# A decoder layer in one kernel: unread products and reordered loads ahead of the first tokens, five instead of four query projections ahead of the output projection

## The reference

```
x = x + attention(layernorm(x))           # 32 query heads, 8 key/value heads, rope, causal, out projection, biases
x = x + quantise(layernorm(x)) @ quantise(ctx[b])      # 0..255 levels, two scales and zero points
x = x + base(layernorm(x)) + lora          # x @ W_org.T + routed mixture: down (8x64), softmax weights, up
```

## Time and profile before

| | us |
|---|---|
| median of 3 runs (lowest, highest) | 791.65 (790.46, 792.01) |
| profiled execution | 793.04 |
| its span | 791.2 |

### The profile page before, as it was taken

One profiled execution on the slowest core, in us unless ns is written; L12 is line 12 of the kernel. 1 busy time (PEld: TensorE's weight loads), 2 busy tenths in 40 slices (PEclk: granted clock), 3 DMA queues, 4 the chain that ended last, 5 costly groups with the idle time before them and its releaser, 6 DMA issues.

```text
span 791.2 us, 12919 instructions
## 1 busy us (share of the span) xinstructions
PE 693.7 (88%) x4608; PEld 556.9 (70%) x4608; DVE 421.7 (53%) x1123; ACT 429.9 (54%) x1025; POOL 307.6 (39%) x384
## 2 busy tenths in 40 slices
PE   3999599999999899998768687799996787799998
PEld 3897477788777677875546475588875666588886
DVE  3366377776777536656648353433336569831212
ACT  3325378878787667797665653646314660512320
POOL 5337655543342534471304710505713011525510
PEclk9998899999999999999979698999999797699999
DMA  7504856563445606225350430403425342323102
GB/s 251 193 2 159 245 174 170 157 172 97 136 121 177 201 23 189 64 75 163 112 164 1 130 75 4 120 14 108 160 88 179 100 148 85 120 93 107 41 13 94
DMA packets 43823, 93.49 MB, mean 118 GB/s; under 512 B 5488, under 2 KB 5872, under 8 KB 42224
## 3 DMA queue, kind: packets, MB, share of 16 engines
q1 hardware_dynamic: 40176, 76.94, 30.2%
q0 software_dynamic: 3584, 15.73, 8.3%
HBM read 72.72 MB, written 19.92 MB: 117 GB/s over the span
## 4 chain that ended last, share of the span: by engine, by line
PE 58%; DVE 15%; POOL 9%; ACT 8%; issue 6%; DMA 2%; SPq 1%; DVEq 0%; ACTq 0%
PE dense L1023 37%; PE probt L917 7%; PE score L905 5%; PE pv L932 4%; POOL w_lo L1558 3%; PE score L1023 2%; DVE stats L1295 2%; DVE prob_all L1251 2%; ACT stage L1060 2%; ACT prob_all L1104 2%; POOL ln_s L828 2%; DVE act_t L1318 1%; POOL prob_all L1575 1%; POOL ln_s L830 1%; DVE prob_all L1344 1%
## 5 line engine op out<-in xcount | busy, mean ns | idle before, releaser
L1023 PE MATMUL dense<-w_hi,act_t 128*128 128x512 f32 (+1 forms) x684 | 233.4, 404 | 23.6 <-DVE act_t L1318 10.7
L1251 DVE CUSTOM_DVE_ANT_0 prob_all<-score,mask_sb 128x128 f32<-128x128 f32 (+3 forms) x256 | 123.7, 487 | 141.4 <-PE score L905 139.5
L1558 POOL TENSOR_TENSOR w_lo<-stage,w_hi 128x512 fp32r<-128x512 f32 x89 | 116.4, 1316 | 191.5 <-ACT w_hi L1064 191.2
L1104 ACT ACTIVATE prob_all<-prob_all,neg_max 128x128 f32<-128x128 f32 (+3 forms) x256 | 143.2, 559 | 72.4 <-DVE neg_max L1251 70.6
L1023 PEld LDWEIGHTS dense<-w_hi,act_t 128*128 128x128 f32 x684 | 133.3, 200 | 51.8 <-DVE act_t L1318 11.8
L1023 PE MATMUL dense<-w_lo,act_t 128*128 128x512 f32 (+1 forms) x372 | 138.5, 393 | 5.6 <-DVE xres L1389 3.1
L1023 PE MATMUL dense<-act_t,w_hi 128*128 128x512 f32 x408 | 139.6, 424 | 1.8 <-DVE xres L1367 1.8
L917 PE MATMUL probt<-ident_sb,prob_all 128*128 128x128 f32 x640 | 113.9, 277 | 1.4 <-ACT prob_all L1113 1.1
L905 PE MATMUL score<-k_stack,q_stack 96*128 96x128 f32 (+3 forms) x256 | 92.1, 364 | 13.9 <-DVE neg_max L1251 7.5
L1064 ACT ACTIVATE w_hi<-stage 128x512 fp32r<-128x512 f32 x117 | 71.9, 624 | 50.9 <-PE dense L1023 31.1
L1113 ACT ACTIVATE prob_all<-probt 128x128 f32<-128x128 f32 (+3 forms) x160 | 68.2, 426 | 47.0 <-PE probt L917 46.0
(11 more groups left out here) (156 smaller groups left out, 916.0 us busy)
## 6 DMA issues: line engine op xcount, KB each, us to landing
q_stack<-rope_dram POOLq DMA_DIRECT2D x16, 768.0 KB, 7.4
stage<-in_w_qk SPq DMA_DIRECT2D x40, 256.0 KB, 3.0
rope_dram<-act_t SPq DMA_DIRECT2D x40, 256.0 KB, 3.3
stage<-in_w_o SPq DMA_DIRECT2D x32, 256.0 KB, 3.0
stage<-in_ctx_kv SPq DMA_DIRECT2D x24, 256.0 KB, 3.1
stage<-in_w_org SPq DMA_DIRECT2D x24, 256.0 KB, 2.8
xres<-in_x SPq DMA_DIRECT2D x8, 512.0 KB, 6.6
prob_all<-in_x SPq DMA_DIRECT2D x8, 512.0 KB, 6.8
```

The costliest lines, as they stand in the source:

```text
L1023: last = engine.matmul(dst, lhs, rhs, start=(k == 0 and c == 0), stop=(k == g.kts - 1 and c == len(pairs) - 1))
L1104: engine.activation(prob[:, u % P_SLOTS, 0:length], prob[:, u % P_SLOTS, 0:length], ACT.Exp, bias=neg_max[:, m:m + 1], scale=-1.0, accum_o ...
L1251: engine.tensor_tensor_reduce(prob[:, u % P_SLOTS, 0:length], score_bank[u % 2][:, 0:length], mask_sb[:, S - length:S], -1.0, HIGHEST, ALU ...
L1558: engine.tensor_tensor(slot_lo(p, 0, NW), raw_of(p), slot_hi(p, 0, NW).bitcast(F32), ALU.subtract).then_inc(g_piece, 1)
```

## The change

- `keep_clock`: PE runs 16 matmuls of 512 columns on a zeroed tile (in q_stack) into dense bank 0 before the first turn. No one reads them.
- Norm (1,0) has its chains on DVE. SP issues the loads of token tiles 1, 2, 3 later, and the key weights earlier. ACT and DVE have tile 0's norm first, and the rest in a new order.
- In slots 0 to 2 the turn of the next token tile stands in the middle of the 24 steps, not behind them.
- The query projection 4 of half 1 stands ahead of `out` 0; before it stood between `out` 0 and `out` 1.
- `PV_LAG`: product with the values one slot later, and with it all that follows (sum's transposes, scaling, attention's parts).
- In units: cross pieces are rounded a slot after their scaling; DVE has the maximum and the probability copy ahead of the token copies. Four low pieces of `base` 0 of half 0 go from POOL to DVE.
- Outside units, a turn needs its source 5.0 us of the plan earlier (`LATE_TURN_US`), not 1.2, so it stands behind more steps; DVE has the second quantising step first in its slot.

```diff
+PV_LAG = 5
+BLANKS = 16
+LATE_TURN_US = 5.0
-CHAINS_ON_VECTOR = ((2, 1), (3, 1))
+CHAINS_ON_VECTOR = ((1, 0), (2, 1), (3, 1))
...
-        for g in range(NKV - LATE_ROPES):
+        for g in range(NKV - LATE_ROPES + 1):
             self.whole("q", 1, g, [0], KD, S, 4)
         self.whole("out", 0, 0, self.TILES, KD, NW, 1)
...
             if cross:
-                self.note("round", j, p)
+                self.note("round", j + 1 if unit else j, p)
...
-        return p < 8 and p % 2 == 1 or ... or piece["kind"] == "out" and p % 2 == 1
+        return p < 8 and p % 2 == 1 or ... or piece["kind"] == "base" and piece["b"] == 0 and piece["nb"] == 0 and p % 2 == 1
...
-                if not self.past(j, source, 3 if unit else 1, now, 1.2):
+                if not self.past(j, source, 3 if unit else 1, now, 1.2 if unit else LATE_TURN_US):
...
             fetch(1)
+            fetch(2)
             load_x(0, 1)
-            fetch(2)
             fetch(3)
-            load_x(0, 2)
             engine.dma_start(bias_v[:, :], b_v.to_broadcast([P, VW])).then_inc(d_bv, 16)
             fetch(4)
             fetch(5)
-            load_x(0, 3)
             fetch(6)
             fetch(7)
+            load_x(0, 2)
+            load_x(0, 3)
...
+            def keep_clock():
+                e.wait_ge(v_blank, 1)
+                for _ in range(BLANKS):
+                    engine.matmul(dense_bank[0][:, :], blank[:, 0:P], blank, start=True, stop=True)
...
-                if j < NT:
+                if j == 0:
+                    keep_clock()
                     for half in range(2):
-                        turn_tokens(1, 0, j, half)
+                        turn_tokens(1, 0, 0, half)
...
                 for s in range(first, end):
+                    if j < NT - 1 and s == first + plan.token_steps // 2:
+                        for half in range(2):
+                            turn_tokens(1, 0, j + 1, half)
...
-                if 0 <= u - 4 < UNITS and (u - 4) % GROUP == GROUP - 1:
-                    values((u - 4) // GROUP)
+                if 0 <= u - PV_LAG < UNITS and (u - PV_LAG) % GROUP == GROUP - 1:
+                    values((u - PV_LAG) // GROUP)
```

More of the change, by code:

```diff
@@ L391, in due_norms @@
                     self.note("turn", j, (which, b, t, half))
-                    self.note("tokens", j + 1 if unit else j, (which, b, t, half))
+                    self.note("tokens", j + TOKENS_LAG if unit else j, (which, b, t, half))
                     halves.append(j)
@@ L1458, in vector_program @@
                 u = j - first_unit
+                if j < NT - 1:
+                    for half in range(2):
+                        tokens_low(1, 0, j + 1, half)
                 if j < NT - 2:
@@ L1461, in vector_program @@
                         norm_stats(1, 0, j + 2, part)
-                if j < NT - 1:
-                    for half in range(2):
-                        tokens_low(1, 0, j + 1, half)
                 if j == NT + 2:
@@ L1468, in vector_program @@
                     constants()
+                if 0 <= u < UNITS:
+                    maximum(u)
+                if 0 <= u - 3 < UNITS and probt_on[u - 3] == "vector":
+                    take_out_turned(u - 3)
+                if not 0 <= u < UNITS:
+                    for b, t in at["second"].get(j, ()):
+                        quantise_second(b, t)
                 for which, b, t, half in at["tokens"].get(j, ()):
```

54 lines of the change are left out of this document (31 added, 23 removed).

## The result

| | before | after |
|---|---|---|
| median of the runs compared (lowest, highest) | 791.83 (790.46, 793.52) | 759.29 (757.09, 764.01) |
| profiled execution, span | 793.04, 791.2 | 760.35, 758.6 |

The ratio is 0.960 [0.954, 0.965], 32.5 us.

What follows compares the result with a forecast made beforehand. PE was taken as full in places, with order able to earn before the units, in their second half and in two norms of half 1. 8.5 + 3 + 4 + 4 + 2.5 = 22 us gave 770, 8-in-10 range 760 to 784.

Steps and rivals of the forecast that it cites:

- Term 1: Start to the first unit: earlier norm chains, mid-slot turns and earlier statistics of half 1 bring score 0 forward 8.5 us.
- rival D: Start: tiles 2 and 3 land late, slots 1 and 2 each wait 3 us, gain only 2.5; 776 us; chance 0.1.
- Term 2: Units to 345 us: later values end PE's copy waits and the earlier query projection fills slots; 3 us.
- Term 3: Units from 345 to 546 us: later rounding and moved low parts remove some 15 us of PE waits; 4 us counted.
- Rival B: Second half of the units opens: rounding apart saves half a microsecond in 30 slots, 12 us not 4; 762; chance 0.2.
- A: Only the start arrives whole; nothing from 345 to 546 us, where ACT is busy, half elsewhere; 778 us; chance 0.2.
- Terms 4 and 5: Late norms of half 1: later turns fill PE's waits in norm (2,1), 4 us; earlier statistics in norm (3,1), 2.5 us.
- Rival C: Late norm: eight turns hold base steps a slot each, PE stands 24 us more, clock falls; 804 us; chance 0.05.

Runs made afterwards that it cites:

- u_blank: The changed kernel without the 16 unread products on PE at the start: 760.6 us, ratio 0.960 to the kernel before.
- u_order: The changed kernel with DVE's token copies ahead of maximum and probability copy again: 761.2 us, ratio 0.964 to the kernel before.
- u_q4: The changed kernel with four query projections of half 1 ahead of `out` 0 again, not five: 753.8 us, ratio 0.954 to the kernel before.
- b_lowround: The kernel before with four low parts of `base` 0 moved to DVE and cross pieces rounded a slot after scaling: 773.6 us, ratio 0.976.
- u_low: The changed kernel with the four low parts of `base` 0 of half 0 on POOL again: 766.9 us, ratio 0.971 to the kernel before.
- u_late: The changed kernel with `LATE_TURN_US` at 1.2 again, not 5.0: 767.6 us, ratio 0.972 to the kernel before.
- u_turn: The changed kernel with the next token tile's turn behind all 24 steps of a slot again: 768.6 us, ratio 0.972 to the kernel before.

## Why the prediction was right and where it was wrong

**Term 1 (8.5, measured 10.0)** went by its steps. ACT's first norm starts at 8.04 (forecast 8.15), PE waits 1.78 at tile 1's turn (2.0), slot 1 starts at 22.80 (23.0 to 23.3), the statistics of half 1 at 38.76 (39.4). Slots 1 to 3 start without a wait, and loads of tiles 2 and 3 were in time: rival D fell. The unread products were priced at 0.3 us, and u_blank shows no more. The Trainium skill, page "TensorE: Matmul & The Clock Gate", section "Why this matters for your kernels", was weighed against them: from it I concluded that v of tile 0 would still be slow. The section speaks of long idle stretches, longer than the one here, so this took it further than it goes. v ran at the upper level in this profile, though PE stood 1.58 and 1.07 us ahead of it:

```profile
9.43 1.06 PE L895 MATMUL probt<-ident_sb,xres 128*128 128x128 f32 x8 [1.58 <-ACT xres L1106]
11.56 0.36 PE L1035 MATMUL dense<-w_hi,act_t 128*128 128x256 f32 x1 [1.07 <-DVE act_t L1340]
```

In u_order's profile it ran slow (0.57 of full speed from 9 to 17 us), behind a stand of 1.87 us. So stands of this length are followed by a fall in some executions and not in others.

**Term 2 (3, measured 3.0)** was right in sum by two wrong parts. The later values earned 3.6, as told, of which 0.9 is work moved past score 176. The fifth projection did fill slots: 378 dense matmuls stand between scores 0 and 136, not 357, in the same 171.0 us. But work that is filled in early earns only if the stretch that loses it gets shorter, and u_q4 shows that it doesn't: 5.9 us are lost by W. And "nothing new waits for it" was wrong for the values: the price stands behind W, on POOL.

**Term 3 (4, measured 12.7) is the step that failed.** It named the right waits, some 15 us, and took "a quarter of those waits, because a wait removed in front of ACT's exponentials comes back in part behind them". The measured term is 12.7: PE stands 7.8 us less, half of those 15 and not a quarter, and 4.8 us are shorter products. Three errors made the size. The clock, 4.8 of the 12.7 us here and 7.2 of the 21.0 in b_lowround, was put at nothing. The share that comes back was guessed from PE's waits, and no row gave it: in the kernel before, rounding later takes 13.5 us off DVE's wait for scaling (23.0 to 9.5) and earns 12.1; in the changed kernel it takes 19.3 off (24.3 to 5.0) and earns 1 to 4. And the low parts were priced as a wait of 7.6 us that shrinks. They are worth 7.6 us of the time, while that wait is 7.7 (7.3 in u_low); most of it is the clock, 6.8 of the 7.9 us of the stretch. Rival B had the size, 12 and 762, and the fewer falls of the clock, and was given 0.2. But it gave all of it to rounding, which is worth 12.1 us in the kernel before and 1 to 4 in the changed one, where the low parts earn more; so its size is in part luck. Its own sum, half a microsecond in 30 slots, is 15 and not 12. The lower end of term 3, four slots of 3 us, is -12 and not -8. ACT's load, the reason for A, was no bound: it is the same 123 us in stretches of 199.8 and 178.8.

The Trainium skill, page "SBUF — State Buffer", section "Who interferes with whom", would have made the low parts on DVE a loss for POOL's chains. Such a collision was seen before, 1.40 us for one step. In b_lowround they meet again, and both sides pay. POOL's first step of a chain takes 0.53 us beside DVE's low part of 425.76, and 0.21 alone; its attention part takes 1.74, and 1.28 alone; DVE's low part beside POOL's of 430.50 takes 1.48, and 0.69 alone:

```profile
426.67 0.53 POOL L821 TENSOR_SCALAR ln_s<-mean_var 128x1 f32<-128x1 f32 x1
...
431.73 1.74 POOL L1569 TENSOR_TENSOR act_t<-inv_wide,act_t 128x512 fp32r<-128x512 f32 x1
...
433.55 0.21 POOL L821 TENSOR_SCALAR ln_s<-mean_var 128x1 f32<-128x1 f32 x1
```

```profile
425.76 1.36 DVE L1231 TENSOR_TENSOR w_lo<-stage,w_hi 128x512 fp32r<-128x512 f32 x1
...
430.84 1.48 DVE L1231 TENSOR_TENSOR w_lo<-stage,w_hi 128x512 fp32r<-128x512 f32 x1
...
440.00 0.69 DVE L1231 TENSOR_TENSOR w_lo<-stage,w_hi 128x512 fp32r<-128x512 f32 x1 [1.95 <-ACT w_hi L1064]
```

So the trace agrees that they collide, but the price on POOL is 0.3 to 0.5 us at these two, not 1.06, and DVE takes four low parts of 1.28 us off POOL: the edit earns 6 to 8 us.

**Terms 4 and 5 (6.5, measured 6.9)** were right in sum, in part by where W stands: some 2.2 of the 6.9 us are the units' small matmuls that the changed kernel does ahead of W, so about 4.7 remain. They would be some 8 without the wait of 3.46 us that the later values put behind W, and u_late gives 8.7 for the turns alone. Their inner sizes were not: I had PE still stand 2.2, 3.8 and 5.9 us before the first three turns, and it stood 2.0, 0 and 0. The 12 us that went came back for the most part: PE's waits for DVE's outputs grew from 4.9 to 8.3 us, the second context sum now waits 4.0 for its pieces, and the low part of `down` 3.5. From W to the end PE stands 24.1 us instead of 26.9, and is busy 4.1 us less, of which 2.2 is the moved work and some 2 the clock.

**Rival C** fell: no stretch grew.

What stays open: how much of rounding's 12 us in the kernel before is the opened circle and how much the moved plan; and why it is worth only 1 to 4 us in the changed one, where the wait of 3.46 us behind W that comes with it is a part of the answer. Also why the fifth projection costs most beside the later values. In these cases the edits meet in the same slots, and no run here separates them.

## What to carry to other kernels

- Look for circles: an engine that waits for a neighbour in the same slot, with the operation behind it feeding that neighbour. Here a slot of distance took 13.5 us off such waits on DVE in one kernel, and 12 off the time; in the other it took 19.3 off the waits and 1 to 4 off the time. So try it, and don't price it by the wait.
- Where PE stands often, an edit earns twice: the standing, and the products that then run at the upper clock. Here this was over a third of term 3 (4.8 of 12.7 us).
- An edit to one operation's slot can move a whole plan, and a stretch between two fixed points then holds other work. Count the instructions in it before comparing.
- Moving an operation later takes all that hangs on it along, and its price can stand hundreds of microseconds behind: read the queues of the last slots. Undo each edit of a bundle by itself; two of these cost 3.6 and 5.5 us inside a gain of 32.5.

## What the runs showed of the hardware

- With PE at the upper clock from its first real product, 1.78 us of standing came with a fall to 1.2 GHz, for 10 to 14 us, in 4 of 8 profiles, and with none in the other four. Stands of 1.10 and 0.98 us came with one as well (u_turn). With the wait cut to 0.34 us there was none in two of two.
- DVE's low part of 128x512 (two SBUF inputs) beside a like operation of POOL: DVE 1.48 us, 0.69 alone; POOL 1.74, 1.28 alone.
- The clock column reads 1.00 from 11 to 17 us in u_blank although its matmuls take as long as at 1.2 GHz: ahead of the first recorded change, the durations tell the level, not the column.
